# Attention tail: the reciprocal row sums spread by a column-tiled matmul, and the output projection in full fp32

## The reference

```python
q, k, v = (proj(Wq, bq), proj(Wk, bk), proj(Wv, bv))       # 8 heads of 32
scores = jnp.einsum('bhqd,bhkd->bhqk', q, k) * SCALE
scores = scores * (adj_matrix + bond_matrix)[:, None, :, :]
attn = jax.nn.softmax(scores, axis=-1)
ctx = jnp.einsum('bhqk,bhkd->bhqd', attn, v)
ctx = ctx.transpose(0, 2, 1, 3).reshape(b, seq_len, EMBED_DIM)
return jnp.einsum('bse,fe->bsf', ctx, Wo) + bo
```

## Time and profile before

| | |
|---|---|
| runs | 3620.78, 3623.7, 3626.34 us, median 3623.7 |
| profiled execution: its time and its span | 3626.3 us both |
| PE busy | 3252.9 us, 90% |
| DVE busy | 2349.3 us, 65% |
| ACT busy | 1824.9 us, 50% |
| chain that ended last, by engine | PE 47%, issue 32%, DVE 9% |
| attention steps, as a stretch of element 5 | 18.5 us a tile, of which PE busy 17.84, DVE 16.39, ACT 15.07 |

### The profile page before, as it was taken

The page is one execution under the profiler, slowest core; times in us unless marked ns, Lnnn a source line. Parts: engine busy times, 40 slices in busy tenths (PEclk is TensorE's granted clock), DMA queues, the critical chain, the costliest instruction groups (busy, mean ns, idle before and its releaser), DMA issues.

```text
span 3626.3 us, 81606 instructions
## 1 busy us (share of the span) xinstructions
PE 3252.9 (90%) x27672; PEld 2797.1 (77%) x27672; DVE 2349.3 (65%) x4108; ACT 1824.9 (50%) x3153; POOL 576.9 (16%) x1677
## 2 busy tenths in 40 slices
PE   6898988999889898898988999789897999988998
PEld 5787778877788777887778877788676887778877
DVE  4736867368673685736857378573786637866377
ACT  3434843358433584335843368433674336743367
POOL 0201112011130111301113011130011200112011
PEclk9999999999999999999999999899998999989999
DMA  2002100031000210002100031000310003100020
GB/s 96 1 1 82 43 31 1 1 85 46 25 1 4 82 46 25 1 7 81 45 24 1 8 87 46 17 1 11 84 46 16 1 13 83 55 7 1 15 66 17
DMA packets 62710, 118.26 MB, mean 33 GB/s; under 512 B 7976, under 2 KB 43565, under 8 KB 62253
## 3 DMA queue, kind: packets, MB, share of 16 engines
q1 hardware_dynamic: 62252, 112.50, 10.5%
HBM read 78.92 MB, written 33.55 MB: 31 GB/s over the span
## 4 chain that ended last, share of the span: by engine, by line
PE 47%; issue 32%; DVE 9%; DMA 4%; POOL 3%; ACT 2%; DVEq 1%; SPq 0%; POOLq 0%; ACTq 0%
PE ps L616 10%; PE ps L428 7%; PE ps L606 7%; PE ps L430 7%; PE ps L429 7%; PE ps L629 5%; DMA qk_spill<-u_lo 2%; DVE t_lo L1037 2%; DMA k_stack<-qk_spill 2%; DVE ev L1190 2%; PE ps L499 1%; PE ps L560 1%; PE ps L644 1%; DVE xt_lo L1044 1%; POOL shift L395 1%
## 5 line engine op out<-in xcount | busy, mean ns | idle before, releaser
L1292 DVE CUSTOM_DVE_ANT_0 r<-ps,adjn 128x1024 f32<-128x1024 f32 x512 | 621.9, 1217 | 31.0 <-PE ps L616 20.8
L984 ACT ACTIVATE r<-r,nmax 128x1024 f32<-128x1024 f32 x512 | 586.9, 1146 | 86.0 <-POOL nmax L420 85.8
L616 PEld LDWEIGHTS ps<-ident,r 128*128 128x128 f32 x4096 | 474.1, 143 | 122.6 <-DVE pt L1301 75.8
L616 PE MATMUL ps<-ident,r 128*128 128x128 f32 x4096 | 555.9, 279 | 6.1 <-DVE pt L1301 6.1
L428 PE MATMUL ps<-u_hi,t_hi 128*128 128x256 f32 x1536 | 449.7, 293 | 72.5 <-DVE t_lo L1037 68.4
L1301 DVE COPY pt<-ps 128x512 f32<-128x512 f32 x512 | 353.2, 690 | 154.2 <-PE ps L616 154.0
L429 PE MATMUL ps<-u_lo,t_hi 128*128 128x256 f32 x1536 | 441.1, 287 | 0.0
L430 PE MATMUL ps<-u_hi,t_lo 128*128 128x256 f32 x1536 | 440.9, 287 | 0.0
L606 PE MATMUL ps<-k_stack,q_stack 96*128 96x512 f32 x1024 | 377.1, 451 | 66.1 <-DVE mmax L1292 34.2
L783 ACT ACTIVATE pt<-ps 128x512 f32<-128x512 f32 x512 | 305.4, 596 | 189.5 <-PE ps L616 184.5
L428 PEld LDWEIGHTS ps<-u_hi,t_hi 128*128 128x128 f32 x1536 | 300.8, 196 | 85.5 <-DVE t_lo L1037 79.7
(11 more groups left out here) (174 smaller groups left out, 6251.6 us busy)
## 6 DMA issues: line engine op xcount, KB each, us to landing
adjn<-in_adj SPq DMA_DIRECT2D x64, 512.0 KB, 3.4
q_stack<-qk_spill SPq DMA_DIRECT2D x24, 512.0 KB, 6.9
k_stack<-qk_spill SPq DMA_DIRECT2D x24, 512.0 KB, 7.4
xn<-in_x SPq DMA_DIRECT2D x16, 512.0 KB, 4.0
x_spill<-xn SPq DMA_DIRECT2D x64, 128.0 KB, 1.7
qk_spill<-u_hi SPq DMA_DIRECT2D x16, 512.0 KB, 6.0
qk_spill<-u_lo SPq DMA_DIRECT2D x16, 512.0 KB, 7.5
xr<-x_spill SPq DMA_DIRECT2D x64, 128.0 KB, 2.1
```

The costliest lines, as they stand in the source:

```text
L616: last = pe.transpose(ps[:, TP + half, t * P:(t + 1) * P], r[:, u % RSLOTS, (TPH * half + t) * P:(TPH * half + t + 1) * P], ident)
L984: act.activation(r[:, s % RSLOTS, :], r[:, s % RSLOTS, :], ACT.Exp, bias=nmax[:, s % 4:s % 4 + 1], accum_out=prow[:, qt % 2, h:h + 1]).the ...
L1292: dve.tensor_tensor_reduce(out=r[:, s % RSLOTS, :], in0=ps[:, 2 * (s % 2):2 * (s % 2) + 2, :].rearrange("p a c -> p (a c)"), in1=adjn[:, q ...
```

## The change

The reciprocals are no longer transposed and spread in two steps. One column of `rprow`, read 32 times over (`broadcast_to`, step zero), is the stationary operand of a matmul with the identity; it writes its transpose into 32 output partitions, and four heads fill 128. The copy `rt`, the constant `sel` and the slot of `spread_denominators` go. The output weight is kept as one fp32 tensor `w_out`, and `output` multiplies the fp32 `c_f` by it directly: two fp32 matmuls instead of six fp32r ones, and no split. The slots move: PE's `output` from step 1 to step 0, DVE's residual block from step 2 to step 1, ACT's `rbc` from step 5 to step 4, ACT's last normalisation from step 5 to 4 and POOL's norm work from step 3 to 2. The loops end a step or more earlier.

```diff
-        w_hi = sb("w_hi", [P, 12, FT, F], F32R)
-        w_lo = sb("w_lo", [P, 12, FT, F], F32R)
+        w_hi = sb("w_hi", [P, 11, FT, F], F32R)
+        w_lo = sb("w_lo", [P, 11, FT, F], F32R)
+        w_out = sb("w_out", [P, FT, F])
...
             for et in range(FT):
-                pe.matmul(ps[:, ACC + 2, 0:F], st_bb[:, 1, et, :], f32(w_hi[:, W_O, et, :]), start=False, stop=False)
-                last = pe.matmul(ps[:, ACC + 2, 0:F], st_bb[:, 1, et, :], f32(w_lo[:, W_O, et, :]), start=False,
+                last = pe.matmul(ps[:, ACC + 2, 0:F], st_bb[:, 1, et, :], w_out[:, et, :], start=False,
                                  stop=(et == FT - 1))
...
-                pe.matmul(ps[0:H, 7, 0:P], rprow[:, qt % 2, :], ident[:, :], start=True, stop=True).then_inc(rt_full, 1)
-
-            def spread_denominators(b, qt):
-                pe.wait_ge(rt_ready, nth(b, NT, qt + 1))
                 for g in range(2):
-                    last = pe.matmul(ps[:, 7, g * P:(g + 1) * P], sel[:, g, :], rt[:, :], start=True, stop=True)
+                    for hh in range(G):
+                        h = g * G + hh
+                        last = pe.matmul(ps[HD * hh:HD * (hh + 1), 7, g * P:(g + 1) * P],
+                                         rprow[:, qt % 2, h:h + 1].broadcast_to([P, HD]), ident[:, :],
+                                         start=True, stop=True, tile_position=(0, HD * hh))
                 last.then_inc(rbc_full, 1)
 
             def output(b, qt):
-                pe.wait_ge(c_ready, nth(b, NT, qt + 1))
+                pe.wait_ge(c_raw, nth(b, NT, qt + 1))
                 for g in range(2):
-                    last = three(ps[:, 7, 0:F], c_hi[:, g, :], c_lo[:, g, :], w_hi[:, W_O, g, :], w_lo[:, W_O, g, :],
-                                 g == 0, g == 1)
+                    last = pe.matmul(ps[:, 7, 0:F], c_f[:, g, :], w_out[:, g, :], start=(g == 0), stop=(g == 1))
                 last.then_inc(o_full, 1)
...
-                    if s >= 13 and (s - 13) % H == 0 and (s - 13) // H < NT:
-                        spread_denominators(b, (s - 13) // H)
-                    if s >= 17 and (s - 17) % H == 0 and (s - 17) // H < NT:
-                        output(b, (s - 17) // H)
+                    if s >= 16 and (s - 16) % H == 0 and (s - 16) // H < NT:
+                        output(b, (s - 16) // H)
...
-                    if s >= 16 and (s - 16) % H == 0 and (s - 16) // H < NT:
-                        qt = (s - 16) // H
-                        dve.wait_ge(c_hi_ready, nth(b, NT, qt + 1))
-                        rest(c_lo[:, :, :], c_f[:, :, :], c_hi[:, :, :], c_ready)
-                    if s >= 18 and (s - 18) % H == 0 and (s - 18) // H < NT:
-                        qt = (s - 18) // H
+                    if s >= 17 and (s - 17) % H == 0 and (s - 17) // H < NT:
+                        qt = (s - 17) // H
                         dve.wait_ge(o_full, nth(b, NT, qt + 1))
                         dve.wait_ge(xr_biased, nth(b, NT, qt + 1))
                         dve.tensor_tensor(xr[:, qt % 2, :], ps[:, 7, 0:F], xr[:, qt % 2, :],
```

More of the change, by code:

```diff
@@ L40, in build_program @@
     COPIES = 2 * G * HALVES
-    W_L0X, W_L0G, W_K0, W_K1, W_K2, W_G1, W_G2, W_G3, W_Q, W_K, W_V, W_O = range(12)
+    W_L0X, W_L0G, W_K0, W_K1, W_K2, W_G1, W_G2, W_G3, W_Q, W_K, W_V = range(11)
     TP_UNITS = 4 * 4 + 3 * HALVES * NT
@@ L141, in build_program @@
             c_f = sb("c_f", [P, 2, P], F32, s)
-            c_hi = sb("c_hi", [P, 2, P], F32R, s)
-            c_lo = sb("c_lo", [P, 2, P], F32R, s)
             rbc = sb("rbc", [P, 2, P], F32, s)
-            rt = sb("rt", [H, P], F32, s)
             xr = sb("xr", [P, 2, F], F32, s)
@@ L369, in _ @@
             pool.memset(zero[:, :], 0.0).then_inc(set_const, 1)
-            pool.wait_ge(set_const, 6)
+            pool.wait_ge(set_const, 5)
             pool.affine_select(out=ident, in_=ident, compare_op=ALU.not_equal, fill=1.0, base=0,
                                pattern=[[-1, P]], channel_multiplier=1).then_inc(set_const, 1)
[L374 to L378, removed]
             def layer_norm(b, layer):
@@ L407, in _ @@
                     layer_norm(b, layer)
-                for u in range(UNITS + 12):
-                    if u >= 19 and (u - 19) % H == 0 and (u - 19) // H < NT:
-                        norm_tile(b, 3, (u - 19) // H)
+                for u in range(UNITS + 11):
+                    if u >= 18 and (u - 18) % H == 0 and (u - 18) // H < NT:
+                        norm_tile(b, 3, (u - 18) // H)
                     if u >= 14 and (u - 14) % H == 0 and (u - 14) // H < NT:
@@ L433, in _ @@
             pe.wait_ge(set_in, SET_LOADS)
-            pe.wait_ge(set_const, 9)
+            pe.wait_ge(set_const, 6)
             bank = lambda n: ps[:, TP + n % 2, :].rearrange("p (k o) -> p k o", o=F)
@@ L450, in _ @@
                                      st_aw[:, dt, :], start=(dt == 0), stop=(dt == FT - 1))
-            pe.wait_ge(set_act, 9)
+            pe.wait_ge(set_act, 8)
             pe.wait_ge(set_dve, 8)
@@ L764, in _ @@
                 scores(b, 0)
-                for s in range(UNITS + 10):
+                for s in range(UNITS + 9):
                     if s + 1 < UNITS:
@@ L786, in _ @@
             act.wait_ge(set_in, SET_LOADS)
-            act.wait_ge(set_const, 9)
-            for n, slot in enumerate((W_L0X, W_L0G, W_Q, W_K, W_V, W_O)):
+            act.wait_ge(set_const, 6)
+            for n, slot in enumerate((W_L0X, W_L0G, W_Q, W_K, W_V)):
                 act.wait_ge(set_pe, n + 1)
@@ L797, in _ @@
             copy(placer[:, 4 * G * HD:], ones[:, 0:2 * HD], 0.0).then_inc(set_act, 1)
-            act.wait_ge(set_act, 8)
+            act.wait_ge(set_act, 7)
             for h in range(G):
@@ L968, in _ @@
                     act.wait_ge(qk_out[k], nth(b, 32, 32))
-                for s in range(UNITS + 14):
-                    if s >= 21 and (s - 21) % H == 0 and (s - 21) // H < NT:
-                        normalise(b, 3, (s - 21) // H)
+                for s in range(UNITS + 13):
+                    if s >= 20 and (s - 20) % H == 0 and (s - 20) // H < NT:
+                        normalise(b, 3, (s - 20) // H)
                     if LAG <= s < UNITS + LAG:
@@ L985, in _ @@
                                        accum_out=prow[:, qt % 2, h:h + 1]).then_inc(exp_done, 1)
[L986 to L991, removed]
+                    if s >= 12 and (s - 12) % H == 0 and (s - 12) // H < NT:
+                        qt = (s - 12) // H
                         act.wait_ge(rbc_full, nth(b, NT, qt + 1))
@@ L995, in _ @@
                         copy(rbc[:, :, :].rearrange("p g q -> p (g q)"), ps[:, 7, 0:2 * P]).then_inc(rbc_ready, 1)
[L996 to L1001, removed]
         @block.vector
@@ L1014, in _ @@
                                          op0=ALU.mult, op1=ALU.subtract).then_inc(set_dve, 1)
+            dve.wait_ge(set_pe, 6)
+            dve.tensor_copy(w_out[:, :, :].rearrange("p k o -> p (k o)"), ps[:, TP + 1, :]).then_inc(set_dve, 1)
             dve.wait_ge(set_pe, 7)
@@ L1017, in _ @@
             dve.memset(st_ab[:, 1:2], 0.0).then_inc(set_dve, 1)
-            dve.wait_ge(set_act, 7)
+            dve.wait_ge(set_act, 6)
             dve.tensor_tensor(w_lo[:, W_K0:W_G3 + 1, :, :].rearrange("p w k o -> p (w k o)"),
@@ L1022, in _ @@
                               ALU.subtract).then_inc(set_dve, 1)
-            dve.wait_ge(set_act, 11)
+            dve.wait_ge(set_act, 10)
             dve.tensor_tensor(wsj_lo[:, :, :], ps[:, PR, 0:2 * FT].rearrange("p (t k) -> p t k", k=2),
@@ L1026, in _ @@
             dve.tensor_reduce(e_const[:, :], ps[:, PR, 8:10], AX.X, ALU.add).then_inc(set_dve, 1)
-            dve.wait_ge(set_act, 12)
+            dve.wait_ge(set_act, 11)
             dve.wait_ge(set_dve, 11)
@@ L1282, in _ @@
                     dve.wait_ge(qk_out[k], nth(b, 32, 32))
-                for s in range(UNITS + 13):
+                for s in range(UNITS + 10):
                     if s < UNITS:
@@ L1306, in _ @@
                         if qt >= 2:
-                            dve.wait_ge(rt_full, nth(b, NT, qt - 1))
+                            dve.wait_ge(rbc_full, nth(b, NT, qt - 1))
                         dve.reciprocal(rprow[:, qt % 2, :], prow[:, qt % 2, :]).then_inc(rp_ready, 1)
```

6 lines of the change are left out of this document (removed).

## The result

The changed kernel takes 3704.1 us (median of 4 runs, 3702.6 to 3705.2) against 3624.9 before: ratio 1.022, 95% interval 1.0206 to 1.0235. It is slower, as forecast, but by 79 us instead of 50, and 4 us above the top of the range. The profiled execution has a span of 3703.4 us, 77.1 more than before.

What follows compares the result with a forecast made beforehand. No engine had much room; transpose-copy round trips, PE's own work and a 5.04 us DVE detour set the tile. (7.2 - 0.25 - 0.5) x 8 - 1.7 = +50 us gave 3674 us, range 3645 to 3700.

Steps and rivals of the forecast that it cites:

- sign: Whole kernel: slower than before, by 1.4%; chance of slower 0.85.
- walk: One attention tile followed from transpose start to transpose start on PE and DVE: distances summing to 19.53 us against 18.27.
- slots moved. This is the part that decides: Attention steps 0 to 3: PE work leaves the shadow of DVE's 5.04 us detour, PE idles 1.8; tile +1.2 us taken.
- The sum: Whole kernel: (7.2 - 0.25 - 0.5) x 8 - 1.7 = +50 us, predicting 3674 us.
- Removed spread: Step 5 of a tile: T5 to T6 falls from 2.18 to the 1.71 us round trip, gain 0.47 us.
- Column-tiled denominators: Step 3 of a tile: 16 records at 25 ns take 0.40 us instead of 0.20.
- The rival with 2.1 us: Step 3: column tiles don't overlap with a step-zero operand, denominators up to 2.1 us, +82 us, 3756; chance 0.04.
- fp32 output: Output projection: two fp32 matmuls take 0.85 us against 0.70 for the six replaced, +0.15 us, between 0.15 and 1.0.
- Start and end of an element: Per element: first tile -0.25 us; end between -1.0 and -0.1, taken as -0.5 us.
- Setup: Setup, once: two matmuls less of 0.85 us at half clock, -1.7 us.
- the clock falls: Attention tile, T3 to T5: PE at 1.2 instead of 2.4 GHz after idling, up to +125 us, 3800; chance 0.05.
- The smaller case: Attention tiles: only a part of the up to 125 us from PE's lower clock, called likelier; no size given.

Runs made afterwards that it cites:

- mirror experiments: Changed kernel with its slots moved back: 3590.0 us, ratio 0.990; kernel before with only the slots moved one step earlier: 3741.3 us, ratio 1.0324.
- fp32 kernel: Kernel before with only the output made two fp32 matmuls of `c_f` at its old slot, no `c_hi` or `c_lo`: 3620.6 us, ratio 0.9987.

## Why the prediction was right, and where it failed

**The sign and the walk.** The step "slots moved. This is the part that decides" held. Undisturbed tiles of the changed kernel are within 0.1 us of the forecast in every distance. The mirror experiments settle the cause: slots alone +3.2%, all but the slots -1.0%.

**The sum.** The walk's terms added up to +50, and without the clock it is +46: that near only because two misses cancel, which is luck. Between the first and the last denominators of an element I had 6 x 1.2 x 8 = 58 and it was 67. My mean of 18.44 left out an element's first period, 17.69, and its last, 15.79; they became 19.64 and 16.28. Outside, I had -8 and it was -21.

**Removed spread.** -0.47 forecast, T5 to T6 fell from 2.18 to 1.71. Right.

**Column-tiled denominators.** 0.40 us forecast. From their start to the scores behind the gap, 826.76 - 826.11 = 0.65, less the gap of 0.20: 0.45. Right to 0.05. The rival with 2.1 us is out.

**fp32 output.** +0.15 forecast; 818.06 to 818.81 is 0.75 to the scores, whose load overlaps, and T0 to T1 grew by 0.87. The fp32 kernel alone grew by 0.16. Right. The Trainium skill (FP8 and Floating Point Precision, TensorE Precision Notes) counts four passes for true fp32; the estimate from it was 0.93 - 0.70 = +0.23. The measured 0.16 lies nearer to the row's 0.15, by little.

**Start and end of an element.** -0.75 us forecast for both. From the last T7 to the next element's first adjacency transposes it was 17.33 before in element 1 (469.26 to 486.59), after it is 493.75 - 477.12 = 16.63. That is the largest difference of all; the medians of the seven passages are 17.00 and 16.66, so -0.34 where I had -0.5. The two ends of that stretch in the changed kernel:

```profile
477.12 0.85 PEld L601 LDWEIGHTS ps<-ident,r 128*128 128x128 f32 x8 [0.89 <-DVE pt L1275]
...
493.75 1.57 PEld L484 LDWEIGHTS ps<-ident,adjn 128*128 128x128 f32 x8 [4.48 <-issue]
```

Setup: -1.7 forecast, -2.6 measured (the first adjacency transposes at 35.2 instead of 37.8 us).

**The step that failed: the clock.** I priced "the clock falls" as a rival with 0.05, on the ground that PE's stops of up to 1 us had left the clock alone, and kept the granted clock at 1.00 in the forecast's sum. The walk itself had found a stop of 1.8 us, which no row of the tile before showed. It lowered the clock in 20 of 48 tiles, 1.5 us each, 31 us. Without it the time would have met the forecast of 3674: the changed kernel with PE kept busy has 3671 to 3674 us (by the two misses above that cancel). The Trainium skill (TensorE: Matmul & The Clock Gate, HAM oscillation) has the mechanism, that stops between bursts of matmuls bring the clock down again and again, and I named it and gave it too little weight. Its case has waits of 3 to 5 us for a DMA; here 1.87 us was enough in 20 of 48 tiles. The upper price of the rival, 125 us, was too high: a fall costs 1.5 us and does not come in every tile. The smaller case, which I had called likelier within the rival, has no term in the sum and no room in the range: 3674 and 31 are 3705, over its top of 3700.

## What to carry to other kernels

Where engines hand work to each other in a fixed step order, cost a change by a walk through one period, start to start, on the engine that waits and the one it waits for. A long block on a helper engine has a shadow, and the work queued on the waited-for engine behind the next wait must lie in it; to make the helper's block earlier can push that work out. And when the walk yields a PE stop longer than any in the profile, give the clock's fall a term of its own in the sum and room in the range, not only a small chance as a rival. Here such a stop lowered the clock 20 and 22 times in 48 in the two kernels that had it; for other lengths and other kernels no run gives the share. A walk through one period doesn't price the ends of the loop; walk them apart.

## What the runs showed of the hardware

A PE stop of 1.87 us in a tile of 19.6 brought the granted clock from 2.4 to 1.2 GHz in 20 of 48 tiles, at 1.5 us each; the same stop filled with identity matmuls, or cut to 0.93 us, in none. Useless matmuls so made a kernel faster by 33 us, 31 of them in the periods. Of 16 column-tiled fp32 records with step-zero stationary operands each costs 28 ns (0.45 us for all), against 25 ns with ordinary ones (0.79 us for the 32 of a context part). The odd delays of 0.17 to 0.36 us in some tiles came and went with small changes of the program (there before and with the column tiles alone, gone in the fp32 kernel and in the kernel with the slots moved back); I have no cause for them.
